# Attention with 16 heads: mask products in two halves of 64 rows, and a sequence's pieces sent behind the rows of maxima

## What is computed

```python
k = (kq @ Wk + bk).reshape(n, T, H, hd).transpose(0, 2, 1, 3)      # T = 256, H = 16, hd = 8
q = (kq @ Wq + bq).reshape(n, T, H, hd).transpose(0, 2, 1, 3)
scores = einsum('bhqd,bhkd->bhqk', q, k) + mask                     # 0 where seen, -inf where not
out = einsum('bhqk,bhkd->bhqd', softmax(scores), vv)
```

## Time and profile before

| what | value |
|---|---|
| runs | 2338.33, 2344.24, 2347.04 us; median 2344.24 |
| the profiled execution | 2333.73 us, span 2331.9 us |
| PE busy over the span | 73% |
| ACT, DVE busy over the span | 37%, 53% |
| granted clock of PE, mean | 0.81 |
| layer 1, 511 to 700 us: PE, DVE, ACT busy of 189 | 145.38, 94.88, 81.43 us; granted clock 0.86 |
| layer 2, 1203 to 1418 us: PE, DVE, ACT busy of 215 | 177.10, 116.91, 93.77 us; granted clock 0.91 |
| layer 3, 1609 to 1800 us: PE, DVE, ACT busy of 191 | 137.20, 101.54, 78.36 us; granted clock 0.83 |

### The profile page before, as it was taken

The page is one execution under the profiler, slowest core; times in us unless marked ns, Lnnn a source line. Parts: engine busy times, 40 slices in busy tenths (PEclk is TensorE's granted clock), DMA queues, the critical chain, the costliest instruction groups (busy, mean ns, idle before and its releaser), DMA issues. The chain is left out here.

```text
span 2331.9 us, 34732 instructions
## 1 busy us (share of the span) xinstructions
PE 1706.5 (73%) x11928; PEld 1171.9 (50%) x11952; DVE 1234.4 (53%) x4310; ACT 869.3 (37%) x1799; POOL 460.1 (20%) x605
## 2 busy tenths in 40 slices
PE   3227844757878786866547987996776776899988
PEld 1106714334545476666433544764343564677666
DVE  4754545324542778875336652333555777666422
ACT  1131223433552356656423554342344331133423
POOL 0000000012200243433024300001220211655311
PEclk8665567657998798987768998987798885899979
DMA  2000000012100454666023200001211000000000
GB/s 82 0 9 1 0 8 20 0 57 56 47 17 6 145 203 162 209 225 217 7 87 83 66 17 10 0 0 56 53 45 36 26 1 1 1 2 3 2 1 19
DMA packets 79739, 115.42 MB, mean 49 GB/s; under 512 B 8416, under 2 KB 60384, under 8 KB 78816
## 3 DMA queue, kind: packets, MB, share of 16 engines
q0 software_dynamic: 18432, 67.38, 8.3%
q1 hardware_dynamic: 58560, 44.87, 7.0%
q10 hardware_dynamic: 2592, 1.18, 0.2%
HBM read 88.82 MB, written 1.05 MB: 39 GB/s over the span
## 5 line engine op out<-in xcount | busy, mean ns | idle before, releaser
L2159 POOL DMA_INDIRECT f_rows<-tree_table,f_index x128 | 131.8, 1030 | 328.3 <-DVE f_index L2215 206.1
L2372 PE MATMUL f_ps_o<-f_rows,shared_sb 128*128 128x128 f32 x1024 | 135.4, 298 | 68.0 <-ACT f_rows L2444 68.0
L2372 PEld LDWEIGHTS f_ps_o<-f_rows,shared_sb 128*128 128x128 f32 x1024 | 131.2, 212 | 73.5 <-ACT f_rows L2444 69.9
L1307 ACT ACTIVATE x_probs<-x_ps_z 128x768 f32<-128x768 f32 (+1 forms) x128 | 117.4, 917 | 132.3 <-PE x_ps_z L1172 72.6
L2444 ACT ACTIVATE f_rows<-f_rows,f_low_act 128x128 f32<-128x128 f32 x512 | 152.9, 386 | 0.8
L2254 DVE CUSTOM_DVE_ANT_0 f_rows<-f_rows,f_xn 128x128 f32<-128x128 f32 x512 | 111.3, 286 | 59.1 <-DMA f_rows<-tree_table,f_index 59.1
L1015 DVE TENSOR_REDUCE x_minus_max<-x_ps_s 128x4 f32<-128x1024 f32 x64 | 78.1, 1224 | 69.8 <-PE x_ps_s L1172 69.6
L1163 PE MATMUL x_ps_z<-x_queries,x_keys 64*128 64x256 bf16 (+1 forms) x512 | 48.4, 269 | 47.5 <-DMA x_queries<-x_max_pieces 29.1
L1632 PE MATMUL f_ps_h<-f_xnT,weights 128*128 128x512 f32 x144 | 76.4, 658 | 2.7 <-ACT f_hT L1697 2.7
L1307 ACT ACTIVATE a_probs<-a_ps_z 128x768 f32<-128x768 f32 x64 | 51.9, 811 | 69.5 <-PE a_ps_z L1169 69.5
L1644 PEld LDWEIGHTS f_ps_y<-weights,f_hT 128*128 128x128 f32 x576 | 70.1, 192 | 14.3 <-issue 12.6
(11 more groups left out here) (624 smaller groups left out, 4317.8 us busy)
## 6 DMA issues: line engine op xcount, KB each, us to landing
x_queries<-x_pieces SPq DMA_DIRECT2D x96, 64.0 KB, 2.1
x_keys<-x_pieces SPq DMA_DIRECT2D x84, 64.0 KB, 2.1
a_queries<-a_pieces SPq DMA_DIRECT2D x48, 64.0 KB, 2.1
weights<-w_L_ffn SPq DMA_DIRECT2D x1, 2985.5 KB, 10.1
a_keys<-a_pieces SPq DMA_DIRECT2D x42, 64.0 KB, 2.0
weights<-w_L_ffn SPq DMA_DIRECT2D x1, 2449.0 KB, 10.6
weights<-w_L_ffn SPq DMA_DIRECT2D x1, 2176.0 KB, 10.5
f_rows<-tree_table,f_index POOLq DMA_INDIRECT x128, 6.0
```

The source lines that it names most:

```text
L1307: a.activation(probs[:, r % HELD, :, :], ps_z[:, :, 0:WIDE], ACT.Exp, scale=scale).then_inc(exped, 1)
L2159: pool.indirect_dma_start(rows[:, u % 2, j, tree, :], None, g.tree_table, bass.IndirectOffsetOnAxis(index[:, u % 2, low, j * TREES + tree: ...
L2372: last = pe.matmul(ps_o[:, low, j, :], g.ident, rows[:, u % 2, j, tree, OUT + f * D:OUT + (f + 1) * D], start=k == 0, stop=k == TREES * FA ...
```

## The change

It does three things in `attention16` and in the layout of the constants.

1. In the causal attentions `hide` adds the mask with four products instead of two. The identity (`eyes`) and the masks now lie in halves: rows 0 to 63 of the mask in part 0, rows 64 to 127 in part 1, each part twice, in rows 0 to 63 and in rows 64 to 127. A head's mask is then the sum of two products of 64 rows, both in the rows of that head. The attention of layer 2 keeps its products of 128 rows.
2. SP sends `stack(u)` one slot later, in slot 8u - 8, and there behind `store_rows(u - 2)`, in all three attentions.
3. The constants become twice as wide: DVE casts `eyes` and each of the four masks with 256 columns instead of 128 before PE may begin, and the weights' DMA carries them.

```diff
-        ident16 = sb("ident16", [P, P], BF16)
         if causal:
-            masks = sb("masks", [P, 4, P], BF16)
+            eyes, masks = sb("eyes", [P, 2, P], BF16), sb("masks", [P, 2, 4, P], BF16)
         else:
+            ident16 = sb("ident16", [P, P], BF16)
...
                 if maxima_in(slot) is not None:
                     store_rows(maxima_in(slot))
-                if v_in(slot) is not None:
-                    stack(v_in(slot))
-                if v_in(slot) == 0:
+                if v_in(slot - 1) is not None:
+                    stack(v_in(slot - 1))
+                if v_in(slot - 1) == 0:
                     for ring in range(1, RINGS):
                         set_constant_rows(ring)
...
             v.wait_ge(g.loaded[name], 16)
-            v.tensor_copy(ident16[:, :], g.ident)
             if causal:
+                by_half = lambda m: w[m].rearrange("p (i k) -> p i k", i=2)
+                v.tensor_copy(eyes[:, :, :], by_half("eyes"))
                 for i, m in enumerate(causal):
-                    last = v.tensor_copy(masks[:, i, :], w[m])
+                    last = v.tensor_copy(masks[:, :, i, :], by_half(m))
                 last.then_inc(const_ready, 1)
             else:
-                v.nop().then_inc(const_ready, 1)
+                v.tensor_copy(ident16[:, :], g.ident).then_inc(const_ready, 1)
...
             def hide(banks, u, kind):
-                for i in range(2):
-                    if causal:
-                        last = pe.matmul(by_parts(banks[:, i, 0:WIDE]), ident16[:, :], masks[:, 2 * kind:2 * kind + 2, :],
-                                         start=False, stop=True)
-                    else:
+                if causal:
+                    for part in range(2):
+                        for i in range(2):
+                            rows = slice(STACK * i, STACK * (i + 1))
+                            last = pe.matmul(by_parts(banks[:, i, 0:WIDE]), eyes[rows, part, :],
+                                             masks[rows, part, 2 * kind:2 * kind + 2, :], start=False, stop=part == 1)
+                else:
+                    for i in range(2):
...
+    by_halves = lambda m: np.concatenate([np.concatenate([half, half], axis=0) for half in (m[0:64], m[64:])], axis=1)
+    eyes = by_halves(np.eye(P, dtype=f))
...
-        "mask0": hide(strict0), "mask1": hide(strict), "mask0T": hide(strict0.T), "mask1T": hide(strict.T),
+        "mask0": by_halves(hide(strict0)), "mask1": by_halves(hide(strict)), "mask0T": by_halves(hide(strict0.T)),
+        "mask1T": by_halves(hide(strict.T)), "eyes": eyes,
...
-        "mask": hide(causal), "maskT": hide(causal.T),
+        "mask": by_halves(hide(causal)), "maskT": by_halves(hide(causal.T)), "eyes": eyes,
```

## The result

The median fell from 2341.53 us (2338.33 to 2347.04, 4 runs) to 2280.36 us (2275.70 to 2286.53, 4 runs), a ratio of 0.9738 [0.9702, 0.9774]. The forecast was 2283 in a range of 2266 to 2306. The profiled execution took 2276.16 us with a span of 2274.3, 57.6 less than the span before.

The account below looks back on a forecast made before the run. The order of SP's queue was taken to bound the causal attentions' units. Gains of 23.5, 6.5 and 31.2 us in layers 1, 2 and 3, together 61.2, gave a forecast of 2283 us, range 2266 to 2306.

Parts of the forecast that it names:

- What bounds the kernel: In the causal attentions, SP's queue order: PE waits for rows of maxima, 23.2, 8.6 and 31.1 us in layers 1 to 3.
- the first shifts: At each attention's first shift, rows of maxima come earlier: 5.8, 6.5 and 6.9 us gained in layers 1, 2 and 3.
- The chain through the pieces: From a score to the next unit's first score, 15.1 or 16.4 us; slots 16 to 56 gain 16.4 and 23.0 us.
- POOL's wait: POOL waits for the pieces to land before splitting the next unit; claimed not to bind, its query split done in time.
- The free periods: Eight slots without waits in the causal attentions, with the new masks: 15.9 us in layer 1, 14.9 in layer 3.
- The late slots: Behind slot 56, some 20 slots bound by ACT in each causal attention start exponentials 0.10 us earlier: 2.0 us each.
- The masks' price: On PE in the causal attentions, four mask products of 64 rows take 0.22 us, what a mask costs now.
- The constants: Before PE begins, five DVE casts of twice the columns cost 0.13 us more each: 0.7 us lost per causal attention.
- (a): Rival, chance 0.10: waits for pieces cost more than their length through a low clock after them; 41 us gained, 2303 us.
- (b): Rival, chance 0.07: mask halves do not run side by side, each mask costs 0.22 us more; 2315 us.
- (c): Rival, chance 0.06: rows come no sooner, or the same wait stands at the pieces; hardly any gain, 2340 us.
- (d): Rival, chance 0.04: products of 64 rows let the tensor engine's clock fall in the causal attentions; slower, 2410 us.

Follow-up runs that it names:

- e2: The kernel before with only the new place of `stack`, the pieces sent behind the rows of maxima, and the old masks; 2292.36 us, ratio 0.9755.
- e1: The changed kernel with the pieces back in their old place in SP's queue, so only the masks in halves are left; 2351.31 us, ratio 1.0008.
- e3: The changed kernel with a second buffer for the pieces, so POOL may split the next unit before the last pieces have landed; 2291.30 us, ratio 0.9742.
- e4: The changed kernel with two buffers of pieces, and zeros and query pieces sent ahead of the rows of maxima, only key pieces behind; 2284.02 us, ratio 0.9743.
- e6: The changed kernel with four more DMAs of 64 KB, whose data nobody reads, in each stack batch; 2341.81 us, ratio 0.9991.
- e10: e4 run once more, unchanged, beside e9; 2288.30 us, ratio 0.9749.
- e9: e4 with masks, identity and casts of the kernel before: two products of 128 rows for each mask; 2294.33 us, ratio 0.9767.
- e5: The changed kernel with the mask's two loops exchanged: both halves of one head, then both of the other; 2295.97 us, ratio 0.9787.
- e8: The changed kernel run once more, unchanged, beside the later experiments; 2297.00 us, ratio 0.9782.

## Why the prediction was right, point by point

**What bounds the kernel: right, and shown.** With the order alone changed (e2) 52 us go, with the masks alone (e1) 2. In the first run the first shifts gained 6.07, 7.33 and 7.04 us in layers 1, 2 and 3, where the prediction had 5.8, 6.5 and 6.9. Layer 2 gained 1.27 more between slots 12 and 16; but that stretch ranges from 9.74 to 11.72 over the kernels with the new order, so this is no term of its own.

**The chain through the pieces: right in number, in layer 1 by luck.** Slots 16 to 56 took 80.86 and 79.38 us, predicted 80.7 and 78.8. In layer 3 the waits of line 1152 came, six of them with 5.9 us, of which 3.1 lie in these slots. In layer 1 the prediction let the pieces hold up half of the periods. The trace has one wait of 0.20 at slot 16 and none at slots 24 to 48: with 1.5 us from the end of the last issue to landing, the pieces were there 0 to 1.1 us before those scores. The periods took 16.34 to 16.70 all the same, and the last 14.56. The prediction said that POOL's wait would not bind; that held, but it said nothing of what else moves with that wait: POOL's split fell upon DVE's split of the maxima, and `weigh` waited for DVE. Without that (e3) the periods are 16.10 to 16.16, and the last 14.03. So a cost of 2.3 us that the prediction lacks stood in for 1.2 us of waiting that hardly came, and it took the last period, some 2 us shorter, to be like the others. In layer 3 this collision is 3.3 of the 5.0 us between the changed kernel and e4 (by e3), the order of the pieces 1.7.

The free periods were near: in e4, where no `score` waits, slots 16 to 56 take 74.33 us in layer 3 (five of 14.9 are 74.5) and 78.57 in layer 1 (five of 15.9 are 79.5), each as four longer periods (15.1 and 16.1) and one of 14.0. How close the chain stands to the bound e6 shows: with four more DMAs every first `score` of a unit waits, in both layers.

**The late slots: the step that failed.** The prediction has "Behind slot 56 there is no chain of pieces" and 2.0 us gained in each. The chain reaches one `score` further: slot 56 is itself the first `score` of the last unit, and it waited 2.10 and 2.00 us for its pieces. In layer 1 PE then ran at 1.2 GHz for some 3 us (0.50 from 641 to 643, after 1.00 up to slot 56), and the part from 56 to 75 got 2.05 us longer in place of 2.0 shorter; in layer 3 it got 0.21 longer. Of the pause itself the late slots gained 1.50 and 1.73 (e1, and again e10 against e9): 0.08 to 0.09 for each of 19 slots, not 0.10 for each of 20. Together 6.3 us of the forecast didn't come.

**The masks' price: right.** 0.22 for four products, the pause of about 0.1 behind them, and the order of neighbours makes no difference (e5). The Trainium skill's figures for back-to-back pairs (TensorE: Matmul & The Clock Gate, Back-to-back issue gap), by which the four would have taken some 0.39 (an estimate), are not what this stream shows; the rule in TensorEngine Tiling (Array Packing), Key Properties, that different tiles can load weights and multiply in parallel is what it does show.

**The constants: 0.5 in place of 0.7.** DVE's casts, to be read against the earlier trace rows:

```profile
509.65 0.47 DVE L1063 CAST x_eyes<-weights 128x256 bf16<-128x256 f32 x1
510.04 1.07 DVE L1065 CAST x_masks<-weights 128x256 bf16<-128x256 f32 x4
511.92 3.47 DVE L1069 MEMSET x_v_ones<- 128x4096 f32 x1 [0.80 <-issue]
```

Five casts are over 1.46 us after the first began, predicted 1.5. Before, five casts were over 1.01 after the first began, so they grew by 0.45, less than I had put. That PE starts later by as much no run here isolates.

**The sum.** Predicted were 61.2 us less in the profiled execution, measured 57.6. The two late parts (6.3 too much) are partly offset by layer 2 (8.4 in place of 6.5) and by some 0.9 of small differences, the constants among them. In the second run of the changed kernel (e8) the attentions gained 52.4 and the medians lie 48.7 apart, so that the first came within 3 us of the forecast is partly luck; the stated range, a gain of 38 to 78, holds both.

**The rivals.** (a), dearer waits by a low clock: refuted for slots 16 to 56, where the clock was 1.00 with waits up to 1.36 us; true of the one wait of 2.10 us in layer 1, but not of the 2.00 us in layer 3. The length of the wait alone doesn't tell. Of the nine waits of 1.46 to 2.23 us at slot 56 in the kernels with the whole batch behind the rows (both runs of the changed one, e2, e3, e5) seven were followed by 0.50, that of 1.46 us among them, and those of 2.00 and 1.85 us in layer 3 of the changed kernel's two runs were not. In e6, where each period has such a wait, the mean clock was 0.91. So the mechanism exists. Its price is seen in the late part of layer 1: above that of e4 (30.82) it is 3.55 us longer in the changed kernel's first run, with a wait of 2.10, and 4.57 in the second, with one of 2.23, so 1.5 and 2.3 beside the wait. (b), halves one after another, is refuted by masks in 0.22; (c), the change without effect, by rows sent 0.03 us after DVE's last piece and 58.8 us gained; (d), a low clock from products of 64 rows, by 1.00 through slots 16 to 56.

## What to carry to other kernels

Where one queue sends both what is wanted at once and what is wanted later, look at the order first: 13 DMAs in front of three small ones cost 52 us here, and the code that moved them is three lines. Then follow the batch that was moved to every consumer, the last unit's as well, and look at what its landing releases on other engines; and cut it, so that only what has to stands behind the urgent part (e4). A pause of an engine is worth something only on the side of the product that another engine waits for: the same masks gave 2 us behind the wait in the queue (e1) and 6 once it was gone (e10 against e9).

## What the runs showed of the hardware

**DVE and POOL hold each other up.** DVE's cast at 576.52 lay under POOL's subtraction (576.44 to 577.11) and ended at 577.25, 0.14 after it, where alone it takes 0.28. DVE's 1030 takes 0.41 alone and up to 0.85 beside POOL; at 576.08 line 1027, with one operand from PSUM, kept its 0.41 though POOL's cast at 575.96 ran beside it. The Trainium skill has the rule (SBUF — State Buffer, Who interferes with whom): an instruction of DVE with two inputs in SBUF, or a cast in a two-port mode, shares a port pair with POOL, and the loser blocks for the whole instruction. These rows agree; in which mode the cast runs the profile doesn't say, and that it is the port and nothing else no run here shows.

**A step of the queue.** A DMA of 64 KB or 8 KB costs SP about 0.6 us to issue, and now and then six of them take 0.3 to 1.3 us more (4.86 and 5.14 in e6, in place of 3.80). Why is open. In layer 3 the six batches together are 1.2 us longer in e8 than in the first run of the changed kernel, and its slots 16 to 56 are 1.1 longer; the 3.1 us in the start-up of layer 2 are not traced.
